# Products with zero weights ahead of TensorE's waits for a scores bank, in a two-layer transformer kernel on one core

## The chip, the cores and the metric

The kernel runs on 1 core of a Trainium2 chip. The metric is the device time of one execution in microseconds (us), as the median of several runs. One profiled execution of the kernel stands beside them: the hardware profiler records each instruction of each engine, with the clock that TensorE was granted. The engines are TensorE (PE in the profile, its weight loads PEld), VectorE (DVE), ScalarE (ACT), GpSimd (POOL) and SyncE (SP), which issues the transfers.

## What is computed

Four images of 1024 tokens with 128 features go through two layers. Each layer is a modulated layer norm, a causal attention with 16 heads of 8 features, a residual, a second modulated layer norm, a mixture of experts, and a residual. Cut to the attentions:

```python
# layer 0
Q, K, V = heads(h), heads(h @ Wk + bk), heads(h @ Wv + bv)   # V has 32 features a head
o = softmax(Q @ K.T + causal) @ V
x = x + ga * (h + gelu(o) @ Wf + bf)
# layer 1: q, k rotated; heads 0 to 5 plain, 6 to 9 hyperbolic, 10 to 15 on normalised q and k
out_a = softmax(q @ k.T / sqrt(8) + causal) @ v
inner = q @ k.T - tq * tk.T
dis   = sqrt(1 / curv) * arccosh(maximum(-curv * inner, 1 + 1e-7))
out_b = softmax(1 / (1e-6 + dis) + causal) @ v
out_c = softmax(sqrt(8) * qn @ kn.T + causal) @ v
```

## The kernel before

**Stages.** The program is a row of blocks, b = 0 to 5, with a barrier of all engines after each. Block b ends layer 1 of image b-2 (its experts), runs a joint attention, and then the rest of layer 0 of image b. In the joint attention the heads go in units of four. In block 0 it has the four units (0, 0) to (0, 3): layer 0 of image 0 alone. In blocks 1 to 3 it has seven units in the order (1, 0), (0, 0), (0, 1), (1, 1), (0, 2), (0, 3), (1, 2): the first number is the layer, and layer 1 belongs to the image before. In block 4 it has (1, 0), (1, 1), (1, 2). The text names a unit so, with its block. The four hyperbolic heads of layer 1 are a guest: its 24 half steps run between the steps of these units, in blocks 1 to 3 at every third step, in block 4 at every step from 2 to 25.

**Steps.** A unit has 12 steps, `STEPS`: a chunk `c` of 512 queries, a block `kb` of 128 keys, and the queries that are not masked, 512, 384, 256 or 128 wide. The widths of a unit's steps add up to 4608 columns. For each position p in the stage TensorE's program runs `scores(p + 1)`, then `values(p)`, then what is left of the side jobs, then, where the guest has a half step, `hyp_scores`.

- `scores` (L745) makes four bf16 products, two to a pair (L756). Each pair goes to two of the banks 0 to 3 of the accumulator memory. `take_banks` (L731) has TensorE wait until the pair of two jobs earlier has been read: by ScalarE's exponential (L1067), or, for a half step of the guest, by VectorE (L1375).
- `values` multiplies the exponentials in `pr` with the values into bank 4 (L797): four fp32 products on 32 columns of the array each, beside one another; the profile counts two MATMULs for each. The first key block of a chunk starts the sum, the last one (`kb == 4 * c + 3`) ends it, and VectorE then copies bank 4 out. In units of layer 0 four more products with a tile of ones put the row sums into bank 5 (L802).
- Side jobs stand between the scores and use the banks 6 and 7 in turn: the "pieces" of the row maxima of a later unit (L683, with the mask's product L686 on the diagonal), which VectorE reduces (L1311); the values of the guest (L714); transposes (L690, L697, L703, L726).

**What sets the order.** Each engine runs its program in the order written. TensorE has one queue: whatever stands behind a waiting product waits too. `side_plan` spreads the side jobs over the positions by their columns. `maskt` is the weight tile with the causal mask; TensorE transposes it once at the start, and VectorE makes the bf16 tile `maskqk` of it. `identb` is the identity in bf16.

Of the kernel before, what the change touches and what calls it, by code (L numbers as in the profile page):

```python
# [7 lines left out]
P = 128  # L8
# [15 lines left out]
HYP_EPS = 1e-06  # L24
NORM_EPS = 1e-24
HYP_UNIT = 3
LOW, HIGH = -3e38, 3e38

HEAD_ORDER = [12, 13, 14, 15, 4, 5, 10, 11, 0, 1, 2, 3, 6, 7, 8, 9]

F32, BF16 = mybir.dt.float32, mybir.dt.bfloat16
# [3 lines left out]
STEPS = []  # L35
# [4 lines left out]
NS = len(STEPS)  # L40
# [28 lines left out]
def layer(b, n):  # L69
    return 1 if n == HYP else UN[b][n][0]  # L70
# [39 lines left out]
NOBODY = -1  # L110
# [14 lines left out]
def hyp_at(b, p):  # L125

    return HYP_POS[b].index(p) if p in HYP_POS[b] else NOBODY
# [20 lines left out]
def std_steps(b):  # L148
    return NS * len(UN[b])
# [154 lines left out]
def adaln_kernel(nc, ins, out):  # L304
    with ExitStack() as ctx:
# [12 lines left out]
        w = {}  # L318
# [34 lines left out]
        weight("maskt", [P, P], ins["maskt"])  # L353
        weight("c", [P, 2 * B], ins["c"])
        cols = w["cols"]

        C_BK, C_BF, C_PB, C_QS, C_COS, C_BV = 0, 1, 2, 4, 5, 8

# [199 lines left out]
        def tensor_program(pe, b):  # L558
# [100 lines left out]
            def attention():  # L659
# [4 lines left out]
                def side_job(kind, g, what):  # L664
# [61 lines left out]
                            mm = pe.transpose(ps[:, bank, t * P:(t + 1) * P], o[:, t * P:(t + 1) * P], w["ident"][:])  # L726
                    mm.then_inc(J.side, 1)

                score_job = [0]

                def take_banks():  # L731

                    n = score_job[0]
                    score_job[0] += 1
                    if n == 0 and b >= 2:
                        pe.wait_ge(fs[1].x, NC)
                    if n >= 2:
                        hyperbolic, i, pair = JOBS[b][n - 2]
                        if hyperbolic:
                            pe.wait_ge(h_arg, i + 1)  # L740
                        else:
                            pe.wait_ge(J.exps, 2 * i + pair + 1)
                    return 2 * (n % 2)

                def scores(g, extra):  # L745
                    n, s = divmod(g, NS)
                    c, kb, q0, wd, diag = STEPS[s]
                    k = K_MAX if has_max(b, n) else PAIRS
                    o0 = q0 - c * CH
                    if s == 0 and has_max(b, n):  # L750
                        pe.wait_ge(J.maxrow[n], 48)
                    for pair in range(2):
                        bank = take_banks()
                        for j in range(2):
                            o = ps[:, bank + j, o0:o0 + wd]
                            mm = pe.matmul(o, kop[0:k, slot(n), 2 * pair + j, kb * P:(kb + 1) * P],  # L756
                                           qop[0:k, slot(n), 2 * pair + j, q0:q0 + wd], start=True, stop=True)
                            if j == 0 and extra and (pair or layer(b, n) == 0):
                                side_job(*extra.pop(0))
                        mm.then_inc(J.scores, 1)  # L760
                        if extra:
                            side_job(*extra.pop(0))
# [51 lines left out]
                for p in range(positions(b) + 1):  # L814
                    extra = jobs_at(p)
                    if p + 1 < steps:
                        scores(p + 1, extra)
                    if p < steps:
                        values(p)
                    for x in extra:  # L820
                        side_job(*x)
                    if hyp_at(b, p) != NOBODY:
                        hyp_scores(hyp_at(b, p))

            def output_projections():
# [1115 lines left out]
        with nc.Block() as block:  # L1941
# [70 lines left out]
            @block.vector  # L2012
            def _(dve):
                chain = [0]

                def link(i):
                    chain[0] += 1
                    i.then_inc(dve_chain, 1)
                    dve.wait_ge(dve_chain, chain[0])

                def modulation(l):
                    dve.wait_ge(s_mm, l + 1)
                    m = mod[:, l].rearrange("p j b -> p (j b)")
                    link(nc.vector.tensor_copy(m, ps[:, 6 + l, 0:6 * B]))
                    for j in (1, 4):
                        ins_ = nc.vector.tensor_scalar(mod[:, l, j], mod[:, l, j], 1.0, None, ALU.add)
                    ins_.then_inc(s_ready, 1)

                def gate_sign(l):
                    for j in (2, 5):  # L2030
                        g = mod[:, l, j]
                        link(nc.vector.tensor_scalar(nr[:, 0, 0:B], g, 0.0, 2.0, ALU.is_ge, ALU.mult))
                        link(nc.vector.tensor_scalar(nr[:, 1, 0:B], nr[:, 0, 0:B], -1.0, None, ALU.add))
                        link(nc.vector.tensor_scalar(nr[:, 2, 0:B], g, -1.0, None, ALU.mult))
                        link(nc.vector.tensor_tensor(nr[:, 0, 0:B], nr[:, 2, 0:B], g, ALU.max))
                        link(nc.vector.scalar_tensor_tensor(out=g, in0=nr[:, 0, 0:B], scalar=0.25,
                                                               in1=nr[:, 1, 0:B], op0=ALU.max, op1=ALU.mult))

                dve.wait_ge(s_first, firsts)
                nc.vector.reciprocal(hyp[:, 0:4], curvb[:]).then_inc(s_ready, 1)  # L2040
                nc.vector.tensor_scalar(consts[:, 6:7], cols[:, C_COS:C_COS + 1], -0.5, None, ALU.mult)
                nc.vector.tensor_copy(identb[:], w["ident"][:])
                dve.wait_ge(x_in, 16)
                for t in range(NT):
                    ins_ = nc.vector.bn_stats(st[:, t, :], xin[:, t, :])
                link(ins_)
                for t in range(NT):
                    ins_ = nc.vector.bn_aggr(mv[:, t, :], st[:, t, :])
                ins_.then_inc(ln_var[0], 1)
                y, z, v = sd[:, 0, :], sd[:, 1, :], mv[:, :, 1]  # L2050
                dve.wait_ge(ln_std[0], 1)
                link(nc.vector.tensor_tensor(z, y, y, ALU.mult))
                link(nc.vector.scalar_tensor_tensor(out=z, in0=v, scalar=LN_EPS, in1=z, op0=ALU.add, op1=ALU.mult))
                link(nc.vector.tensor_scalar(z, z, -0.5, 1.5, ALU.mult, ALU.add))
                link(nc.vector.tensor_tensor(z, z, y, ALU.mult))
                dve.wait_ge(ln_tok[1], 1)
                for t in range(NT):
                    nc.vector.tensor_scalar(xin[:, t, :], xin[:, t, :], mv[:, t, 0:1], sd[:, 1, t:t + 1],
                                            ALU.subtract, ALU.mult).then_inc(ln_norm[0], 1)
                modulation(0)  # L2060
                nc.vector.tensor_copy(maskqk[:], ps[:, 6, P:2 * P])
                for c in range(NC):
                    nc.vector.tensor_copy(chunk(xT(0), c), ps[:, c, :])
                gate_sign(0)
                modulation(1)
                gate_sign(1)
# [95 lines left out]
```

## Time and profile before

| | |
|---|---|
| median of 3 runs | 2625.94 us (2622.81 to 2629.74) |
| the profiled execution | 2617.08 us, span 2615.4 us |
| TensorE busy | 2163.1 us, 83% of the span |
| VectorE busy | 1485.9 us, 57% |
| ScalarE busy | 1354.2 us, 52% |
| GpSimd busy | 822.0 us, 31% |
| TensorE's clock granted | 0.821 of full on average |

The clock is granted at two levels, 1.2 and 2.4 GHz; a figure between 0.5 and 1 is the mix of both over a stretch, so that 2 x (1 - figure) is the share of the stretch at 1.2 GHz. The busy time of TensorE counts each product to the modelled end of its pipeline, so a busy TensorE is not yet one that streams at its peak. The profiled execution lies 8.9 us under the median.

### The profile page before, as it was taken

To read this page: it belongs to the slowest core of one execution; us is meant where nothing else is said; L and a number is where in the kernel's file an instruction comes from. 1 tells how busy PE (TensorE), PEld (TensorE's weight loads), DVE (VectorE), ACT (ScalarE), POOL (GpSimd) and SP (SyncE) were. 2 spreads that over 40 slices of the span, in tenths; PEclk is the share of its full clock that TensorE was granted. 3 is DMA by queue.
4 is the path that set the end of the run, shared out by engine and by line. 5 is a ranking of instruction groups with operands and counts; after the bars stand their busy time and mean duration, and the time that the engine had idled before them with its cause. 6 is when DMAs were issued, how large, how long until landed. Compare 5 with 4: busy or idle time off the path is not lost. (4 is left out here: it accounts for less than half of the span.)

```text
span 2615.4 us, 30040 instructions
## 1 busy us (share of the span) xinstructions
PE 2163.1 (83%) x10649; PEld 841.0 (32%) x10649; DVE 1485.9 (57%) x3046; ACT 1354.2 (52%) x1924; POOL 822.0 (31%) x918
## 2 busy tenths in 40 slices
PE   6898938888888499888898949988888868978779
PEld 2233412322224343222223424322222334422133
DVE  6562526667745454666763643576766444388542
ACT  2345415657773232657676422365777532278922
POOL 2112111333431243323342134232344113346624
PEclk7899956887888699687887969778788878976789
DMA  5000241111012242101102234201001223310032
GB/s 131 21 24 18 66 118 30 36 38 27 17 50 82 63 131 75 35 19 36 27 17 66 67 93 128 63 20 31 24 20 49 66 78 96 89 40 1 1 98 89
DMA packets 82104, 142.56 MB, mean 55 GB/s; under 512 B 11821, under 2 KB 34477, under 8 KB 77325
## 3 DMA queue, kind: packets, MB, share of 16 engines
q1 hardware_dynamic: 81954, 140.63, 19.1%
q8 instruction: 85, 1.39, 0.2%
q14 instruction: 65, 0.53, 0.1%
HBM read 124.22 MB, written 15.20 MB: 53 GB/s over the span
## 5 line engine op out<-in xcount | busy, mean ns | idle before, releaser
L1311 DVE TENSOR_REDUCE mx<-ps 128x1 f32<-128x512 f32 (+3 forms) x992 | 613.0, 655 | 281.7 <-PE ps L686 190.1
L1067 ACT ACTIVATE pr<-ps 128x1024 f32<-128x1024 f32 (+3 forms) x672 | 521.7, 804 | 416.0 <-PE ps L756 414.7
L683 PE MATMUL ps<-kop,qop 72*128 72x512 bf16 (+7 forms) x1248 | 447.6, 388 | 95.8 <-DVE mx L1311 69.3
L756 PE MATMUL ps<-qop,kop 75*128 75x512 bf16 (+7 forms) x1344 | 440.3, 383 | 88.2 <-DMA qop<-mrow 35.0
L797 PE MATMUL ps<-pr,vt 128*32 128x512 f32 (+3 forms) x2688 | 358.1, 612 | 10.8 <-POOL pr L1612 8.9
L1612 POOL TENSOR_SCALAR_AFFINE_SELECT pr<-pr 128x512 f32<-128x512 f32 x224 | 158.5, 708 | 617.9 <-ACT pr L1067 615.8
L1120 ACT ACTIVATE pr<-ps 128x512 f32<-128x512 f32 x224 | 133.7, 597 | 308.9 <-PE ps L881 242.9
L683 PEld LDWEIGHTS ps<-kop,qop 72*128 72x128 bf16 (+1 forms) x1248 | 131.4, 107 | 450.7 <-DVE mx L1311 288.6
L756 PEld LDWEIGHTS ps<-qop,kop 75*128 75x128 bf16 (+1 forms) x1344 | 130.7, 109 | 337.7 <-ACT pr L1067 103.0
L891 PE MATMUL ps<-pr,qop 128*128 128x512 f32 x384 | 194.6, 593 | 4.1 <-POOL pr L1603 4.1
L686 PE MATMUL ps<-maskqk,identb 128*128 128x128 bf16 x832 | 194.3, 256 | 0.0
L802 PE MATMUL ps<-pr,ones 128*32 128x512 f32 (+3 forms) x1536 | 178.6, 539 | 0.0
L1603 POOL TENSOR_TENSOR pr<-on,wb 128x512 f32<-128x512 f32 x84 | 106.3, 1265 | 129.1 <-DVE on L1539 123.3
L1539 DVE TENSOR_TENSOR on<-pr,ps 128x512 f32<-128x512 f32 x84 | 57.7, 687 | 149.0 <-ACT pr L1120 148.7
L878 PE MATMUL ps<-hT,kop 128*128 128x512 f32 x256 | 131.0, 593 | 4.3 <-DVE on L1539 4.3
L1375 DVE TENSOR_SCALAR wb<-ps 128x1024 f32<-128x1024 f32 (+3 forms) x96 | 91.6, 954 | 75.2 <-PE ps L770 61.3
L881 PE MATMUL ps<-hT,nbc 128*128 128x512 f32 x256 | 130.7, 592 | 0.0
L1365 DVE COPY osb<-ps 128x512 f32<-128x512 f32 x56 | 38.6, 689 | 127.1 <-PE ps L802 92.3
L891 PEld LDWEIGHTS ps<-pr,qop 128*128 128x128 f32 x384 | 72.3, 190 | 97.7 <-issue 83.1
L1702 POOL TENSOR_TENSOR wb<-wb 128x768 f32<-128x768 f32 (+2 forms) x42 | 76.3, 1816 | 78.7 <-ACT wb L1041 77.3
L686 PEld LDWEIGHTS ps<-maskqk,identb 128*128 128x128 bf16 x832 | 94.9, 114 | 18.5 <-issue 13.5
L797 PEld LDWEIGHTS ps<-pr,vt 128*32 128x32 f32 x2688 | 57.9, 118 | 127.2 <-issue 93.3
(332 smaller groups left out, 3076.9 us busy)
## 6 DMA issues: line engine op xcount, KB each, us to landing
wb<-gates_scratch SPq DMA_DIRECT2D x192, 256.0 KB, 3.3
kop<-kparts_scratch SPq DMA_DIRECT2D x32, 576.0 KB
qop<-qparts_scratch SPq DMA_DIRECT2D x96, 192.0 KB
nbc<-hmax_scratch SPq DMA_DIRECT2D x14, 512.0 KB, 4.3
xin<-in_x SPq DMA_DIRECT2D x7, 512.0 KB, 6.1
kparts_scratch<-on SPq DMA_DIRECT2D x12, 256.0 KB, 3.4
qparts_scratch<-on SPq DMA_DIRECT2D x12, 256.0 KB, 4.0
qparts_scratch<-wb SPq DMA_DIRECT2D x12, 192.0 KB
```

The source lines that it names most:

```text
L683: mm = pe.matmul(o, qop[0:k, slot(n), j, qb * P:(qb + 1) * P], kop[0:k, slot(n), j, k0:k0 + wd], start=True, stop=not diag)
L686: mm = pe.matmul(o[:, wd - P:wd], identb[:], maskqk[:], start=False, stop=True)
L756: mm = pe.matmul(o, kop[0:k, slot(n), 2 * pair + j, kb * P:(kb + 1) * P], qop[0:k, slot(n), 2 * pair + j, q0:q0 + wd], start=True, stop=True)
L797: mm = pe.matmul(ps[32 * j:32 * j + 32, 4, o0:o0 + wd], v, pr[:, g % 3, j, o0:o0 + wd], start=kb == 0, stop=last, tile_position=(0, 32 * j))
L802: mm = pe.matmul(ps[32 * j:32 * j + 32, 5, o0:o0 + wd], ones32[:], pr[:, g % 3, j, o0:o0 + wd], start=kb == 0, stop=last, tile_position=(0 ...
L878: mm = pe.matmul(ps[:, f.gate_banks[i % R], :], wt, h, start=True, stop=True)
L881: mm = pe.matmul(ps[:, 4 + i % 2, :], wt, h, start=True, stop=True)
L891: pe.matmul(ps[:, c, :], wt, fh[:, i % 3, :], start=i < NC, stop=i == f.last[c]).then_inc(g.down, 1)
L1067: nc.scalar.activation(pr[:, g % 3, 2 * pair:2 * pair + 2, o0:o0 + wd], ps[:, bank:bank + 2, o0:o0 + wd], ACT.Exp).then_inc(J.exps, 1)
L1120: nc.scalar.activation(fa[:, i % 3, :], ps[:, f.gate_banks[i % R], :], fn).then_inc(g.act, 1)
L1311: ins_ = nc.vector.tensor_reduce(mx[:, ring(b, n), j0:j0 + heads, qb, col % 2], ps[:, bank, 0:heads * wd].rearrange("p (j n) -> p j n", j= ...
L1612: nc.gpsimd.affine_select(past, past, [[0, 4], [1, P]], ALU.is_ge, 0.0, base=0, channel_multiplier=-1).then_inc(J.cut, 1)
```

## The change

The change adds matrix products that change no sum. Their weights are zeros: the memory of `maskt`, read as bf16 and cleared by VectorE after its only use. Their moving operand is `identb`, repeated to 512 columns. They add to bank 4, where the values' sum is open, so they stand only where the last values step was not the last of its chunk. There are two of them (`FILL`) ahead of each of the two pairs of a step of layer 1, one ahead of each pair of a step of layer 0 two positions after a half step of the guest, and one ahead of each half step of the guest. Block 0 has none.

```diff
@@
+FILL = 2
@@
+        zeros = w["maskt"][:].bitcast(BF16)[:, 0:P]
@@
+                def add_zeros(times):
+
+                    for _ in range(times):
+                        pe.matmul(ps[:, 4, :], zeros, identb[:].unsqueeze(1).broadcast_to([P, 4, P]),
+                                  start=False, stop=False)
+
+                def keep_busy(p, times):
+
+                    if 0 <= p < std_steps(b) and b:
+                        c, kb = STEPS[p % NS][:2]
+                        if kb != 4 * c + 3:
+                            add_zeros(times)
@@ def scores
                     for pair in range(2):
+                        if layer(b, n) or hyp_at(b, g - 2) != NOBODY:
+                            keep_busy(g - 2, FILL if layer(b, n) else 1)
                         bank = take_banks()
@@ position p
                     if hyp_at(b, p) != NOBODY:
+                        keep_busy(p, 1)
                         hyp_scores(hyp_at(b, p))
@@ VectorE, once at the start
-                nc.vector.tensor_copy(maskqk[:], ps[:, 6, P:2 * P])
+                link(nc.vector.tensor_copy(maskqk[:], ps[:, 6, P:2 * P]))
+                nc.vector.memset(zeros, 0.0)
```

TensorE's order at one full step of block 1, unit (1, 0), is this before; L756 are the scores, L683 the pieces, L797 the values:

```order
L683 MATMUL ps<-kop,qop 128x512
L756 MATMUL ps<-qop,kop 128x512 x2
L683 MATMUL ps<-kop,qop 128x512
L756 MATMUL ps<-qop,kop 128x512
L683 MATMUL ps<-kop,qop 128x512
L756 MATMUL ps<-qop,kop 128x512
L683 MATMUL ps<-kop,qop 128x512
L797 MATMUL ps<-pr,vt 32x512 x4
```

The same place in the changed program, where L734 is the product with zeros, L773 the scores, L685 the pieces and L814 the values:

```order
L685 MATMUL ps<-kop,qop 128x512
L734 MATMUL ps<-identb,w_maskt 128x512 x2
L773 MATMUL ps<-qop,kop 128x512 x2
L685 MATMUL ps<-kop,qop 128x512
L734 MATMUL ps<-identb,w_maskt 128x512 x2
L773 MATMUL ps<-qop,kop 128x512
L685 MATMUL ps<-kop,qop 128x512
L773 MATMUL ps<-qop,kop 128x512
L685 MATMUL ps<-kop,qop 128x512
L814 MATMUL ps<-pr,vt 32x512 x4
```

Four rows of 512 columns have come in, two ahead of each pair, and nothing else has moved.

In a unit of layer 0 of block 1 TensorE's order around a half step of the guest (L770) is this before, with the row sums at L802 and the guest's values at L714:

```order
L802 MATMUL ps<-pr,ones 32x512 x4
L683 MATMUL ps<-kop,qop 128x384
L686 MATMUL ps<-maskqk,identb 128x128
L770 MATMUL ps<-qop,kop 128x256 x2
L756 MATMUL ps<-qop,kop 128x512
L714 MATMUL ps<-wb,vt 32x384 x4
L756 MATMUL ps<-qop,kop 128x512
L683 MATMUL ps<-kop,qop 128x384
L686 MATMUL ps<-maskqk,identb 128x128
L756 MATMUL ps<-qop,kop 128x512
```

And in the changed program, where the guest's half step is L787:

```order
L819 MATMUL ps<-pr,ones 32x512 x4
L685 MATMUL ps<-kop,qop 128x384
L688 MATMUL ps<-maskqk,identb 128x128
L734 MATMUL ps<-identb,w_maskt 128x512
L787 MATMUL ps<-qop,kop 128x256 x2
L734 MATMUL ps<-identb,w_maskt 128x512
L773 MATMUL ps<-qop,kop 128x512
L716 MATMUL ps<-wb,vt 32x384 x4
L773 MATMUL ps<-qop,kop 128x512
L685 MATMUL ps<-kop,qop 128x384
L688 MATMUL ps<-maskqk,identb 128x128
L734 MATMUL ps<-identb,w_maskt 128x512
```

One row stands ahead of the half step and one ahead of the next pair; that pair was already the next thing in the queue. By the whole order the changed program has 610 of these products: 158 in each of the blocks 1 to 3 and 136 in block 4.

## Rows read from the trace of the kernel before

**Rows 1.** The page: TensorE's busy time, and its granted clock in 40 slices.

```profile
PE 2163.1 (83%) x10649; PEld 841.0 (32%) x10649; DVE 1485.9 (57%) x3046; ACT 1354.2 (52%) x1924; POOL 822.0 (31%) x918
...
PEclk7899956887888699687887969778788878976789
```

**Rows 2.** Windows, one a unit: block 0's (0, 1), then block 1's seven.

```profile
core 0: us, PE busy (x) PEld busy (x) DVE busy (x) ACT busy (x) POOL busy (x), PEclk, DMA share, GB/s
125.00:167.30 42.30, 39.41 (x322) 14.01 (x321) 25.97 (x47) 20.73 (x28) 7.63 (x10) 1.00 0.12 30
397.90:461.90 64.00, 53.40 (x260) 17.41 (x260) 43.63 (x76) 33.59 (x47) 14.49 (x15) 0.66 0.05 18
461.90:515.00 53.10, 47.22 (x343) 16.41 (x341) 36.48 (x66) 35.60 (x52) 18.89 (x26) 0.91 0.10 24
515.00:575.70 60.70, 50.65 (x374) 17.42 (x372) 40.73 (x79) 35.61 (x56) 17.36 (x23) 0.92 0.14 38
575.70:634.40 58.70, 47.79 (x261) 15.71 (x253) 43.08 (x68) 43.58 (x51) 23.55 (x21) 0.78 0.09 21
634.40:694.50 60.10, 52.96 (x354) 17.46 (x357) 41.69 (x66) 43.95 (x52) 23.20 (x22) 0.84 0.13 30
694.50:746.80 52.30, 47.72 (x340) 16.15 (x333) 36.54 (x61) 38.16 (x53) 21.34 (x27) 0.88 0.08 22
746.80:776.20 29.40, 27.02 (x178) 7.09 (x176) 6.71 (x20) 25.10 (x42) 10.56 (x19) 0.77 0.38 108
```

**Rows 3.** Windows: block 2's (1, 0), (0, 1), (1, 1), (1, 2); block 3's (1, 0), (1, 1).

```profile
1022.10:1089.20 67.10, 56.74 (x269) 18.55 (x268) 44.95 (x78) 33.43 (x45) 14.49 (x15) 0.67 0.14 41
...
1141.00:1207.10 66.10, 56.71 (x374) 19.18 (x372) 41.28 (x79) 35.73 (x57) 17.38 (x23) 0.82 0.13 35
1207.10:1271.30 64.20, 53.35 (x269) 17.39 (x261) 45.56 (x68) 43.79 (x52) 23.14 (x21) 0.70 0.08 20
...
1381.50:1410.90 29.40, 28.20 (x178) 7.27 (x176) 6.65 (x19) 25.03 (x41) 10.25 (x18) 0.71 0.38 108
1657.10:1725.00 67.90, 57.59 (x269) 19.14 (x268) 45.26 (x78) 33.43 (x45) 14.48 (x15) 0.64 0.14 40
...
1841.70:1900.70 59.00, 49.35 (x261) 16.96 (x253) 43.11 (x68) 43.47 (x51) 23.95 (x21) 0.75 0.08 21
```

**Rows 4.** Windows: block 4's (1, 0), (1, 1), (1, 2).

```profile
2283.60:2354.00 70.40, 54.19 (x264) 17.19 (x265) 56.42 (x96) 50.97 (x79) 30.49 (x34) 0.72 0.12 39
2354.00:2445.10 91.10, 70.69 (x319) 21.11 (x317) 75.70 (x104) 82.88 (x97) 59.27 (x47) 0.61 0.00 1
2445.10:2483.80 38.70, 30.43 (x198) 7.70 (x190) 14.32 (x35) 36.37 (x58) 20.92 (x31) 0.79 0.00 0
```

**Rows 5.** Windows: steps 4 to 6 of unit (1, 1), block 1, then block 2.

```profile
594.50:606.20 11.70, 10.40 (x61) 3.23 (x60) 10.07 (x16) 11.53 (x13) 4.15 (x3) 0.85 0.00 1
1225.90:1243.90 18.00, 17.25 (x71) 5.11 (x63) 13.18 (x17) 11.97 (x14) 3.74 (x3) 0.52 0.00 1
```

**Rows 6.** What TensorE waited for in block 1's joint attention: total, times, longest.

```profile
PE ps L683 <- DVE mx L1311: 17.0, 37, 1.5
PE ps L756 <- DVE wb L1375: 7.2, 10, 1.2
PE ps L756 <- DMA qop<-mrow: 7.2, 4, 2.7
PE ps L756 <- ACT pr L1067: 5.2, 8, 1.3
```

**Rows 7.** TensorE's timeline in block 1's (1, 1): start, length, line.

```profile
601.87 0.38 PE L683 MATMUL ps<-kop,qop 72*128 72x512 bf16 x1
602.09 0.38 PE L756 MATMUL ps<-qop,kop 75*128 75x512 bf16 x1
...
603.04 1.07 PE L797 MATMUL ps<-pr,vt 128*32 128x512 f32 x8
604.04 0.28 PE L683 MATMUL ps<-kop,qop 72*128 72x256 bf16 x1
```

**Rows 8.** The same timeline in block 2's (1, 1).

```profile
1230.05 0.63 PE L683 MATMUL ps<-kop,qop 72*128 72x512 bf16 x1
1230.48 0.63 PE L756 MATMUL ps<-qop,kop 75*128 75x512 bf16 x1
```

## The prediction

> **What bounds the kernel now.** I read the page first. TensorE is busy for 83% of the span, far more than any other engine, so the kernel is TensorE's nearly everywhere. But its granted clock is 0.821 on average, and in the 40 slices it is lowest in the joint attentions of the blocks from 1 on (6 to 8 tenths) and in a few phases where other engines work [rows 1]. Next I cut the attentions into units by the windows view and looked at the clock column. Block 0's attention, layer 0 alone, holds 1.00. In block 1 the units of layer 0 have 0.84 to 0.92, those of layer 1 only 0.66 and 0.78, and the last unit 0.77 [rows 2]. Blocks 2 and 3 repeat this: 0.67 and 0.64 for (1, 0), 0.70 and 0.75 for (1, 1) [rows 3]. In block 4 the figures are 0.72, 0.61 and 0.79, but there ScalarE is busy 82.88 us of 91.1 in the longest unit [rows 4]. So in blocks 1 to 3 TensorE sets the pace together with VectorE, which it feeds with pieces, and in block 4 it is mostly ScalarE.
>
> Does the clock matter for the time? The same work recurs at other clocks, and this is the best view of the case. Time at the low clock is 2 x (1 - clock) x length. Unit (1, 1) took 58.7 us with 25.8 us of it at the low clock in block 1, and 64.2 us with 38.5 us in block 2 [rows 2, 3]: 5.5 us more for 12.7, or 0.43 us for each. Unit (0, 1) gives (66.1 - 60.7) / (23.8 - 9.7) = 0.38. Three steps alone took 11.7 us at clock 0.85 and 18.0 us at 0.52 with the same work [rows 5]: 6.3 us for 13.8, or 0.46. Unit (1, 0) gives less, (67.9 - 67.1) / (48.9 - 44.3) = 0.17, and the last unit nothing: 29.4 us at 0.77 and at 0.71, with ScalarE busy 25.1 us of it. I take 0.4 for each us at the low clock, 0.3 in unit (1, 0), 0 in the last unit.
>
> Which waits are there? In the whole attention of block 1 TensorE is idle for 17.0 us on VectorE's reductions, and ahead of scores (L756) for 7.2 us on VectorE's read for the guest, 5.2 us on ScalarE and 7.2 us on a transfer; no wait exceeds 2.7 us [rows 6]. So the waits for a scores bank are few. What the zero products can bring is the clock, not the waits.
>
> **What a product with zeros costs.** It is a bf16 product of 512 columns, as the pieces and scores are. Two such stand 0.22 us apart at the full clock (601.87 to 602.09) [rows 7] and 0.43 us at the low one (1230.05 to 1230.48) [rows 8]. It waits for nothing, needs no other engine, and delays what stands behind it in TensorE's queue: a pair of scores, then a piece. The 158 of a block fall as follows, by the rule on `kb` and the guest's places: 38 in (1, 0), 43 in (1, 1), 41 in the last unit, 36 in the four units of layer 0.
>
> How much of that delay reaches the time? A comparison bounds it from below. A unit of layer 0 has the row sums' products on top of what a unit of layer 1 has: about as long as the values' own, which take 1.00 us in a full step with the changeover (603.04 to 604.04) [rows 7]. At 4608 columns, nine full steps' worth, that is 8 to 9 us a unit. Brought to the full clock by the prices above, the four units of layer 0 in block 1 take 49.3, 56.8, 52.4 and 47.3 us, mean 51.4; (1, 1) takes 48.4 and (1, 0) 51.0, mean 49.7 [rows 2]. So 8 to 9 us of more work on TensorE cost 1.7 us: one fifth. The cover is VectorE, busy 43 us of a unit's 59 to 64, and ScalarE. The upper bound is everything. The zeros stand ahead of the scores, which feed ScalarE, where the row sums stand behind the values and feed nobody at once; so I double the fifth and take 0.4.
>
> **Term A, (1, 0) and (1, 1) of blocks 1 to 3: the clock.** Four zero products in a step are 0.88 us, which is what the row sums add to a step of layer 0. So I forecast for these units the clock that layer 0's have, 0.88 (0.82 to 0.92 in rows 2 and 3). At 60 us that leaves 14.4 us at the low clock in each. Now it is 43.5, 44.3 and 48.9 us in (1, 0), together 136.7, and 25.8, 38.5 and 29.5 in (1, 1), together 93.8 [rows 2, 3]. The fall is 93.5 x 0.3 = 28 us and 50.6 x 0.4 = 20 us: -48 us.
>
> **Term B, their zeros.** 81 a block, 243 in three, x 0.22 = 53.5 us of TensorE; x 0.4 = +21.4 us (between 10.7 and 53.5).
>
> **Term C, layer 0's units of blocks 1 to 3.** 108 x 0.22 = 23.8 us. These units are nearer to TensorE's bound, so half of it, +11.9 us. At the low clock are 9.6 + 9.7 + 19.2 + 12.6 = 51 us in block 1 [rows 2]; I take the same for each block, and a quarter of it to go, since only every third step has zeros: 153 x 0.25 x 0.4 = -15.3 us. Together -3.4 us.
>
> **Term D, the last unit of blocks 1 to 3.** 41 zeros, 9 us of TensorE in a unit of 29.4 us that the clock doesn't move. ScalarE covers nearly all; I take a tenth of 27 us, +3 us (0 to 27).
>
> **Term E, block 4.** 136 x 0.22 = 30 us, covered by ScalarE and VectorE: a tenth, +3 us. At the low clock are 39.4, 71.1 and 16.3 us [rows 4], 127 in all; two thirds of it may go, at a price between 0 (as in the last unit) and 0.4. The longest unit can win at most the 8.2 us that ScalarE is idle in, so I take 0.1: -8.4 us. Together -5.4 us.
>
> **The start.** VectorE now waits for its cast of the mask and clears 128 x 64 words, once. The trace has no such clear; it lies between nothing and a few tenths of a us, and I take +0.3.
>
> Sum: -48 + 21.4 - 3.4 + 3 - 5.4 + 0.3 = -32 us. Against the profiled execution's 2617.1 us that is 2585; against the median of 2625.9, to which the result will be compared, 2594 us.
>
> The Trainium skill, in "TensorE: Matmul & The Clock Gate", section "HAM oscillation — how this bites in real kernels", makes the clock fall after TensorE has been idle for one whole period of the monitor. By that rule fillers in a queue without long gaps can't help. The trace speaks against it: TensorE waits at most 2.7 us at a time in block 1's attention [rows 6] and is busy 53.4 us of 64.0 at clock 0.66 [rows 2]. The same page's next section, "A second HAM failure mode: psum-queue depth-cycling", says that short idles between groups of products make the clock go up and down, and that fits these rows. By the first rule the result is that of the first rival below, by the second that of the forecast.
>
> **Rivals.**
> - *The clock doesn't answer* to products with zeros, or not to work of this kind; the zeros are pure load. At the mix of clocks now they cost about 0.35 us in layer 1's units and 0.25 in layer 0's: 243 x 0.35 x 0.4 = 34, 108 x 0.25 x 0.5 = 13.5, and a tenth of 123 x 0.3 and 136 x 0.35, 8.5. That is +56 us, 2682 us. For it: busy shares of 83% and more at low clocks, so being busy alone doesn't raise it [rows 2]. Against it: the units with the row sums have the higher clock in every block. Chance 0.12.
> - *The zeros hold up what VectorE and ScalarE wait for.* The clock rises as forecast, but each zero product delays the next pair and the piece behind it in full. All 610 at 0.22 us are 134 us, against gains of 48 + 15 + 8 = 72: +62 us, 2688 us. It decides from an exposed share of 0.54 on. For it: VectorE and ScalarE are fed through the same queue; against it: the fifth measured on the row sums. Chance 0.08.
> - *Half a clock.* The low clock shrinks to 0.80 in layer 1's units, 24 us in each: 65 x 0.3 + 22 x 0.4 = 28 us of gain, less 21.4, and no gain in C and E beyond their cost: about -7 us, 2619 us. For it: the last steps of a chunk, and those after them, get no zeros, and unit (1, 0) has waits which zeros don't fill. Chance 0.15.
> - *More than forecast.* The full clock in layer 1's units with a fifth exposed: 137 x 0.4 + 94 x 0.43 = 95 us, less 11, and C to E as above: some -90 us, 2536 us. Chance 0.05.
>
> **How the numbers follow.** The forecast has 0.60, with its own range 2562 to 2616 (exposed share 0.2 to 0.6, clock 0.84 to 0.92). What a measurement of this kernel can tell from no change is about 0.3%, or 8 us. Faster takes the forecast (0.60), more than forecast (0.05) and a third of the half clock (0.05): 0.70. Same takes most of the rest of the half clock and the edge of the forecast's cases: 0.12. Slower takes the first two rivals, less a part that ends near zero: 0.18. The range that leaves out the two dear rivals' centres and the far gain is 2552 to 2640 us.
>
> **What would show it.** In the changed kernel's windows: the clock of (1, 0) and (1, 1) in blocks 1 to 3 near 0.88, their lengths shorter by some 4 to 5 us each net; the last unit at 29 to 31 us whatever its clock; block 0 as before, its clock 1.00. In the waits, less idle time of TensorE ahead of pieces, more of VectorE on TensorE. The forecast is wrong if the clock of these units stays at 0.64 to 0.78 (first rival), or if it rises and the units don't shorten (second). Then ScalarE's and VectorE's waits for TensorE's scores and pieces would have grown.

## The result, and the profile after

The changed kernel took 2608.61 us (median of 4 runs, 2604.3 to 2611.8), the kernel before in the same comparison 2624.55 us. The ratio is 0.9935, with a 95% interval of 0.9914 to 0.9956: 0.65% or 17 us faster, between 12 and 23 (the two medians lie 15.9 us apart). The forecast was 32 us. The profiled execution of the changed kernel took 2611.8 us, its span is 2610.1 us.

From the page of the changed kernel, the busy times and the granted clock in 40 slices:

```profile
PE 2178.3 (83%) x11259; PEld 889.0 (34%) x11259; DVE 1490.6 (57%) x3047; ACT 1355.6 (52%) x1924; POOL 817.8 (31%) x918
...
PEclk7899957988999599998899869898899968988879
```

610 more products stand on TensorE, 134 us of them at 0.22 us each, and its busy time has grown by only 15 us [rows 1]. The others stream faster: the mean clock of the profiled executions went from 0.821 to 0.875.

The windows of the changed kernel, one a unit: block 1's seven, then (1, 0), (0, 0), (1, 1) and (1, 2) of block 2, then block 4's three. They answer to [rows 2, 3, 4].

```profile
398.00:466.80 68.80, 59.21 (x306) 22.73 (x306) 43.82 (x76) 33.72 (x47) 14.07 (x15) 0.74 0.05 16
466.80:516.40 49.60, 44.18 (x350) 15.64 (x342) 36.48 (x66) 35.60 (x52) 18.87 (x26) 1.00 0.10 26
516.40:579.40 63.00, 54.52 (x375) 19.08 (x376) 40.99 (x79) 35.75 (x56) 17.37 (x23) 0.89 0.14 37
579.40:637.40 58.00, 50.07 (x309) 19.17 (x308) 43.10 (x68) 43.67 (x52) 23.20 (x21) 0.89 0.08 22
637.40:695.20 57.80, 51.42 (x367) 17.66 (x366) 42.37 (x66) 43.55 (x52) 23.92 (x22) 0.90 0.14 31
695.20:746.50 51.30, 46.83 (x347) 17.00 (x340) 36.72 (x61) 38.19 (x53) 21.46 (x28) 0.93 0.08 22
746.50:777.40 30.90, 29.50 (x217) 10.12 (x215) 6.54 (x21) 25.18 (x41) 10.26 (x18) 1.00 0.38 103
1025.50:1090.10 64.60, 54.03 (x316) 21.51 (x314) 45.12 (x79) 33.68 (x45) 13.60 (x15) 0.88 0.15 42
...
1090.10:1141.20 51.10, 45.51 (x341) 16.12 (x342) 36.43 (x66) 35.60 (x52) 18.86 (x26) 0.97 0.10 25
...
1204.10:1262.00 57.90, 49.55 (x300) 18.83 (x292) 43.09 (x68) 43.58 (x51) 23.21 (x21) 0.89 0.09 22
1371.30:1402.20 30.90, 29.50 (x217) 10.10 (x215) 6.53 (x21) 25.18 (x42) 10.12 (x18) 1.00 0.37 103
2272.30:2342.20 69.90, 54.41 (x310) 20.40 (x311) 57.65 (x96) 50.85 (x78) 30.29 (x34) 0.89 0.12 39
2342.20:2432.40 90.20, 68.73 (x360) 23.48 (x359) 74.36 (x104) 82.85 (x96) 58.56 (x48) 0.80 0.00 1
2432.40:2475.60 43.20, 37.36 (x240) 11.51 (x238) 14.29 (x35) 36.47 (x58) 20.30 (x30) 0.90 0.00 1
```

Read the column PEclk first: layer 1's units stand at 0.88 and 0.89 where they had 0.67 and 0.70 in block 2, and the last unit at 1.00. Only (1, 0) of block 1 stays low, at 0.74. The lengths follow only in part. In block 2, (1, 0) is 2.5 us shorter and (1, 1) 6.3, the last unit 1.5 us longer. In block 4 the last unit grew from 38.7 to 43.2 us.

TensorE's timeline in a full step of the changed kernel's (1, 1) of block 2 shows one reason:

```profile
1231.25 0.39 PE L685 MATMUL ps<-kop,qop 72*128 72x512 bf16 x1 [0.37 <-DVE mx L1329]
1231.47 0.60 PE L734 MATMUL ps<-identb,w_maskt 128*128 128x512 bf16 x2
1231.91 0.60 PE L773 MATMUL ps<-qop,kop 75*128 75x512 bf16 x2
1232.34 0.38 PE L685 MATMUL ps<-kop,qop 72*128 72x512 bf16 x1
1232.56 0.60 PE L734 MATMUL ps<-identb,w_maskt 128*128 128x512 bf16 x2
1232.99 0.38 PE L773 MATMUL ps<-qop,kop 75*128 75x512 bf16 x1
```

The products with zeros (L734) are where the order put them. Two take 0.44 us (1231.47 to 1231.91), 0.22 each as forecast. But the scores behind them start the moment they end, and so does everything up to 1232.99: there was no wait for a bank for them to fill. In such a step TensorE is the path.

The waits of TensorE in block 1's attention (total, times, longest), which answer to [rows 6]:

```profile
PE ps L685 <- DVE mx L1329: 18.4, 37, 1.5
PE ps L773 <- ACT pr L1085: 4.9, 10, 1.3
PE ps L773 <- DMA qop<-mrow: 4.0, 2, 2.2
...
PE ps L773 <- DVE wb L1393: 1.4, 3, 0.7
```

The wait on VectorE's read for the guest went from 7.2 to 1.4 us: some of the added products stand in such waits and cost nothing there. That on VectorE's reductions grew by 1.4 us.

Added up over the whole span, the two profiled executions differ so:

| part | forecast | before | changed | difference |
|---|---|---|---|---|
| (1, 0) and (1, 1), blocks 1 to 3 (terms A, B) | -26.6 | 381.0 | 371.7 | -9.3 |
| layer 0's units, blocks 1 to 3 (C) | -3.4 | 683.3 | 669.6 | -13.7 |
| the last units, blocks 1 to 3 (D) | +3 | 88.1 | 94.2 | +6.1 |
| block 4's attention (E) | -5.4 | 200.2 | 203.3 | +3.1 |
| everything else | +0.3 | 1262.8 | 1271.4 | +8.6 |

The single parts are less sure than the whole. The execution profiled before was 9 us faster than its median and the changed one 3 us slower. What lies outside the joint attentions, where the program adds nothing but the clear at the start, takes 1103.8 to 1116.0 us in the profiled executions of all kernels of this study.

### The profile page after: what moved, and what is told of

Read it like the earlier page. It is cut to its first block and busy times, and to the rows that moved or that the text cites. A ratio compares the mean times of both kernels' runs of the same rounds, so it can differ in the third digit from the quotient of the medians.

```text
span 2610.1 us, 31253 instructions
## 1 busy us (share of the span) xinstructions
PE 2178.3 (83%) x11259; PEld 889.0 (34%) x11259; DVE 1490.6 (57%) x3047; ACT 1355.6 (52%) x1924; POOL 817.8 (31%) x918
## 5 line engine op out<-in xcount | busy, mean ns | idle before, releaser
L685 PE MATMUL ps<-kop,qop 72*128 72x512 bf16 (+7 forms) x1248 | 418.4, 364 | 98.7 <-DVE mx L1329 73.4
L773 PE MATMUL ps<-qop,kop 75*128 75x512 bf16 (+7 forms) x1344 | 408.9, 353 | 50.2 <-ACT pr L1085 17.7
L814 PE MATMUL ps<-pr,vt 128*32 128x512 f32 (+3 forms) x2688 | 314.7, 542 | 6.7 <-POOL pr L1630 4.9
L685 PEld LDWEIGHTS ps<-kop,qop 72*128 72x128 bf16 (+1 forms) x1248 | 127.8, 104 | 406.1 <-DVE mx L1329 285.7
L734 PE MATMUL ps<-identb,w_maskt 128*128 128x512 bf16 x610 | 212.8, 414 | 16.7 <-DMA qop<-mrow 16.7
L773 PEld LDWEIGHTS ps<-qop,kop 75*128 75x128 bf16 (+1 forms) x1344 | 129.7, 103 | 260.9 <-issue 66.7
L688 PE MATMUL ps<-maskqk,identb 128*128 128x128 bf16 x832 | 184.6, 245 | 0.0
L819 PE MATMUL ps<-pr,ones 128*32 128x512 f32 (+3 forms) x1536 | 165.2, 502 | 0.0
L1654 POOL TENSOR_SCALAR sd<-mv 128x4 f32<-128x4 f32 x30 | 6.9, 229 | 287.3 <-DVE mv L1195 220.3
```

Source lines behind the costliest of these rows:

```text
L685: mm = pe.matmul(o, qop[0:k, slot(n), j, qb * P:(qb + 1) * P], kop[0:k, slot(n), j, k0:k0 + wd], start=True, stop=not diag)
L688: mm = pe.matmul(o[:, wd - P:wd], identb[:], maskqk[:], start=False, stop=True)
L734: pe.matmul(ps[:, 4, :], zeros, identb[:].unsqueeze(1).broadcast_to([P, 4, P]), start=False, stop=False)
L814: mm = pe.matmul(ps[32 * j:32 * j + 32, 4, o0:o0 + wd], v, pr[:, g % 3, j, o0:o0 + wd], start=kb == 0, stop=last, tile_position=(0, 32 * j))
L819: mm = pe.matmul(ps[32 * j:32 * j + 32, 5, o0:o0 + wd], ones32[:], pr[:, g % 3, j, o0:o0 + wd], start=kb == 0, stop=last, tile_position=(0 ...
```

## The experiments

Each kernel is the changed one with the edit shown. The ratios are to the kernel before, with their 95% intervals; 0.9935 is the changed kernel's. All added products leave the sums as they are, so every kernel computes the whole output.

**Is it the streaming?** Each product cut to 8 columns:

```diff
-                        pe.matmul(ps[:, 4, :], zeros, identb[:].unsqueeze(1).broadcast_to([P, 4, P]),
-                                  start=False, stop=False)
+                        pe.matmul(ps[:, 4, 0:8], zeros, identb[:, 0:8], start=False, stop=False)
```

> The changed kernel with its 610 products with zeros cut from 512 to 8 columns; the instructions and their places stay. Theory 1 (the products pay by keeping TensorE streaming, which lifts the granted clock): the clock falls back to about 0.82 and the time to the kernel before's, ratio 1.000 within 0.003, unit (1, 1) of block 2 back near 64 us. Theory 2 (the products pay by the instructions themselves or by where they shift the queue, the clock being incidental): the ratio stays at 0.993 or falls below.

Measured: 1.0028 (1.0001 to 1.0055), median clock of its ten runs 0.8145 against 0.816 before. Two windows of (1, 1), blocks 2 and 3:

```profile
1222.30:1281.70 59.40, 48.93 (x304) 17.50 (x292) 43.26 (x68) 43.60 (x52) 23.59 (x21) 0.77 0.09 21
1864.00:1929.50 65.50, 55.63 (x300) 18.88 (x292) 45.57 (x68) 43.94 (x51) 23.15 (x21) 0.67 0.08 19
```

The same 610 instructions in the same places bring nothing when they stream next to nothing. Clock and gain are gone together. Theory 2 is refuted. But block 2's (1, 1) took 59.4 us and not the 64 expected, block 3's 65.5: one unit of one execution is a poor measure.

**Which products carry it?** Only the pairs' products of layer 1:

```diff
-                        if layer(b, n) or hyp_at(b, g - 2) != NOBODY:
-                            keep_busy(g - 2, FILL if layer(b, n) else 1)
+                        if layer(b, n):
+                            keep_busy(g - 2, FILL)
...
-                        keep_busy(p, 1)
```

> Only the two products ahead of each pair of layer 1's units (116 a block); those at the guest's half steps and in layer 0's units are left out. The changed kernel took 14 us off layer 0's units of blocks 1 to 3 where I had put 3. If that came from the 36 products in them, it is gone here: ratio about 0.998. If it came from the phase in which layer 0's units are entered (the clock's state left by the unit before), most of it stays: 0.994.

Measured: 0.9983 (0.9958 to 1.0009), clock 0.8665. By the profiled execution, the four units of layer 0 take 230.3, 227.0 and 228.4 us in the blocks 1 to 3; before it was 226.2, 228.0 and 229.1, and 221.7, 223.2 and 224.6 in the changed kernel. Without the 36 products in these units the 14 us are gone, as the first reading had it. But the 14 us don't stand firm: the sum of the three blocks is 683.3 us before and 669.6 in the changed kernel, and in other kernels below that keep the 36 products it is 672.0 to 685.0 in their profiled executions.

Only the single products:

```diff
-                        if layer(b, n) or hyp_at(b, g - 2) != NOBODY:
-                            keep_busy(g - 2, FILL if layer(b, n) else 1)
+                        if layer(b, n) == 0 and hyp_at(b, g - 2) != NOBODY:
+                            keep_busy(g - 2, 1)
```

> Only the single products, 42 in each of blocks 1 to 3 and 20 in block 4; none ahead of layer 1's pairs. Theory 1: layer 0's units in blocks 1 to 3 keep a clock over 0.90 and are 3 to 5 us a block shorter than before, units (1, 0) and (1, 1) are at 0.65 to 0.78 as before, and the last units are back to 29.4 us (38.8 in block 4), since their products cost 1.5 and 4.4 us: ratio 0.993 to 0.996. If the two per pair carry the gain, the ratio is 0.998 to 1.000.

Measured: 0.9963 (0.9929 to 0.9997), clock 0.8295: 146 products, a quarter of them, bring some half of the gain by the ratio. The interval is wide, and the two medians differ by only 3.9 us. The windows of the last units of blocks 1 and 2, and of (1, 1) of block 2:

```profile
746.80:775.80 29.00, 25.71 (x179) 7.00 (x177) 6.66 (x19) 24.96 (x41) 10.75 (x19) 0.82 0.41 110
1384.60:1411.00 26.40, 24.30 (x179) 6.56 (x177) 6.74 (x19) 24.60 (x41) 9.79 (x17) 0.87 0.44 120
1210.10:1275.00 64.90, 54.00 (x264) 18.40 (x256) 45.63 (x68) 44.02 (x51) 23.05 (x21) 0.69 0.08 19
```

(1, 1) is back at 0.69 and 65 us, as expected. Layer 0's units come to 226.3, 226.6 and 225.4 us, only 1 us a block or so under before, where 3 to 5 had been expected. By these executions either kind alone gives them little; whether both together give more isn't shown, since the 14 us are one execution.

**What does a product cost where it can't bring anything?** Two ahead of each pair of block 0 as well, at a clock that is 1.00 already:

```diff
-                    if 0 <= p < std_steps(b) and b:
+                    if 0 <= p < std_steps(b):
...
-                        if layer(b, n) or hyp_at(b, g - 2) != NOBODY:
-                            keep_busy(g - 2, FILL if layer(b, n) else 1)
+                        if layer(b, n) or b == 0 or hyp_at(b, g - 2) != NOBODY:
+                            keep_busy(g - 2, FILL if layer(b, n) or b == 0 else 1)
```

> The changed kernel, with two products ahead of each pair in block 0 as well (156 more, 34 us at 0.22 us each). There the clock is 1.00 already, so that only their price shows. If a fifth to two fifths is exposed, as taken in the prediction, block 0's units (0, 1) and (0, 2) grow from 41.6 us by 2 to 4 us and the whole by 7 to 14 us; if TensorE's queue is the path there, they grow by 8 to 9 us each and the whole by about 30 us.

Measured: 0.9982 (0.9958 to 1.0006). The windows of block 0's (0, 1), (0, 2), (0, 3):

```profile
129.80:176.00 46.20, 45.87 (x363) 18.40 (x362) 26.39 (x47) 21.09 (x29) 7.64 (x10) 1.00 0.12 27
176.00:222.10 46.10, 45.76 (x362) 18.36 (x361) 26.39 (x47) 20.99 (x28) 7.63 (x10) 1.00 0.09 24
222.10:256.30 34.20, 33.79 (x272) 11.68 (x274) 1.38 (x2) 20.65 (x28) 7.01 (x9) 1.00 0.01 2
```

In the kernel before, (0, 2) and (0, 3) took:

```profile
167.30:208.90 41.60, 39.47 (x322) 14.01 (x321) 25.98 (x47) 20.77 (x29) 7.63 (x10) 1.00 0.10 27
208.90:236.10 27.20, 25.96 (x234) 7.99 (x236) 1.38 (x2) 20.13 (x28) 7.01 (x9) 1.00 0.01 2
```

So 40 products cost 4.5 us in (0, 2), 0.11 us each or half of their 0.22. In (0, 3), which has no pieces for VectorE, they cost 7.0 us, 0.18 each or four fifths. (0, 1) grew by 3.9 us. The expectations for these two units were 2 to 4 and 8 to 9 us each, so the first nearly held there, and it held for the whole: 0.9982 against 0.9935 is 12 us. This is the purest price of the study.

**Without them in the last units:**

```diff
-                    if 0 <= p < std_steps(b) and b:
+                    if 0 <= p < std_steps(b) and b and p < std_steps(b) - NS - 2:
```

> The changed kernel without the products of the last unit of blocks 1 to 4. There they cost: 29.4 became 30.9 us (32.4 once) and 38.8 became 43.2 us, while with single products alone these units took 26.4 to 29.0 and 40.5 us. Theory 1: the last units fall to 27 to 29 us and to 39 to 41, the rest stays, the whole is 8 to 14 us under the changed kernel, ratio 0.989 to 0.991. Rival: the products keep the clock up into the phases that follow, whose time grows by as much; ratio 0.993 to 0.995.

Measured: 0.9898 (0.9861 to 0.9934), as theory 1 had it for the whole, some 10 us under the changed kernel. The intervals overlap; on the same chip the kernel with zeros by zeros (below), which has the changed kernel's products, had a median of 2608.96 us and this one 2596.35. The profiled last units of blocks 1 to 3 and of block 4:

```profile
748.30:779.80 31.50, 30.16 (x178) 7.80 (x176) 6.70 (x20) 25.31 (x42) 10.48 (x19) 0.67 0.36 101
1376.30:1402.90 26.60, 24.46 (x178) 6.51 (x176) 6.67 (x20) 24.84 (x41) 10.52 (x19) 0.87 0.43 119
1997.30:2028.90 31.60, 28.66 (x178) 7.71 (x176) 6.69 (x20) 25.27 (x42) 10.73 (x19) 0.73 0.36 101
...
2429.10:2468.60 39.50, 33.54 (x198) 7.99 (x190) 14.31 (x35) 36.58 (x58) 20.92 (x32) 0.69 0.00 1
```

The same work takes 26.6 us at 0.87 and 31.5 at 0.67. The last unit does answer to the clock. It fell to the 27 to 29 us expected in block 2 alone; in blocks 1 and 3 it lost the clock with the products and took 31.5 and 31.6. Blocks 1 to 3 together have 89.7 us here, 94.2 in the changed kernel and 88.1 before. (1, 1) of block 4 took 85.2 us at 0.88, where the changed kernel's profile has 90.2 at 0.80 with one product more.

**How many?** First one ahead of each pair, then four:

```diff
-FILL = 2
+FILL = 1
```

> FILL = 1: one product ahead of each pair of layer 1's units, half the load. Theory 1 with the price measured in block 0 (0.115 us of time for each): the price falls by 58 a block and about 6 us a block; if one product is enough to hold the clock of (1, 1) over 0.85 the ratio is about 0.987, if the clock falls back to 0.75 or so it is 0.993 to 0.996.

> FILL = 4. The clock of the units (1, 0) and (1, 1), already 0.88 and 0.89, can rise by 0.1 at most, about 12 us less at the low clock, worth 3 to 5 us a unit; two times 40 more products cost a unit 9 us at the price of block 0, up to 17 us if TensorE's queue is then the path. Units (1, 0) and (1, 1) grow by 4 to 12 us each, the whole by 40 us or more: ratio 1.01 to 1.02.

Measured: 0.9896 (0.9861 to 0.9931) with one and 1.0161 (1.0114 to 1.0209) with four; clock 0.864 and 0.891. One is better than two by 10 us, between the two cases expected; the intervals overlap, but three of the four executions with one lie under all ten of the kernel with zeros by zeros on the same chip. In the profiled execution the clock of (1, 1) fell back in two blocks (0.78 and 0.76, 62.0 us) and not in the third (0.96, 53.9 us). Four raise the clock little and make it dear. Their whole came as expected, by other units than expected: (1, 1) of blocks 1 to 3 grew by only 3 us, under the 4 to 12, and the last units by 5 to 9. The last unit of block 2 with one:

```profile
1379.20:1407.00 27.80, 25.62 (x198) 8.42 (x196) 6.82 (x21) 24.85 (x41) 10.28 (x19) 1.00 0.42 114
```

and that of block 1 with four, with (1, 1) of block 3:

```profile
747.40:785.60 38.20, 37.55 (x255) 13.90 (x253) 6.54 (x21) 25.75 (x42) 10.02 (x18) 1.00 0.30 83
1857.30:1917.80 60.50, 53.92 (x358) 21.88 (x356) 43.40 (x68) 44.03 (x51) 23.00 (x21) 1.00 0.08 21
```

The last unit's rows are at clock 1.00, and so is the changed kernel's at 30.9 us: 27.8 us with one, 30.9 with two, 38.2 with four. The 20 products from one to two cost 0.16 us each, the 40 from two to four 0.18. With one it takes 27.8 us in all three blocks; with none it took 29.3 to 29.4 before, and 31.5, 26.6 and 31.6 in the kernel above.

**Do the data matter?** Zeros as the moving operand too:

```diff
-                        pe.matmul(ps[:, 4, :], zeros, identb[:].unsqueeze(1).broadcast_to([P, 4, P]),
+                        pe.matmul(ps[:, 4, :], zeros, zeros.unsqueeze(1).broadcast_to([P, 4, P]),
```

> The changed kernel with zeros as the moving operand too, in place of the repeated identity: no operand bit changes in the added products. If the granted clock follows the streaming alone, clock (0.88 in units (1, 0) and (1, 1)) and time (ratio 0.993) stay; if it follows what the data switch, the clock of these units falls back toward 0.65 to 0.78 and the time to 1.00 or above.

Measured: 0.9934 (0.9911 to 0.9957), clock 0.879 against 0.8785. (1, 1) of block 1 and (1, 0) of block 2:

```profile
580.80:636.30 55.50, 46.88 (x320) 18.13 (x318) 43.01 (x68) 43.73 (x51) 23.35 (x21) 0.99 0.10 23
1024.10:1088.10 64.00, 53.04 (x316) 20.89 (x314) 45.11 (x79) 33.56 (x45) 13.62 (x15) 0.89 0.15 43
```

Nothing changed: zeros streamed against zero weights hold the clock as well as the identity does. The weights are zeros in both kernels, so products that switch real data in the array were not tried.

**Did (1, 0) gain?** No products in it:

```diff
-                        if layer(b, n) or hyp_at(b, g - 2) != NOBODY:
+                        if UN[b][n] != (1, 0) and (layer(b, n) or hyp_at(b, g - 2) != NOBODY):
...
-                        keep_busy(p, 1)
+                        if p >= NS:
+                            keep_busy(p, 1)
```

> The changed kernel without any added product in the units (1, 0) of blocks 1 to 4 (38 fewer in each of blocks 1 to 3, more in block 4). The prediction put 28 us of gain less 10 of price into these units of blocks 1 to 3; the changed kernel showed 1 us. Theory 1a (a long part of (1, 0) isn't paced by TensorE, so that its clock pays little there): these units stay at 64 to 68 us as before and as with the products, and the whole is within 5 us of the changed kernel, ratio 0.992 to 0.995. Theory 1b (the products there also hold the clock for the unit behind them): unit (0, 0), 49.6 to 51.1 us with them, goes back to 52 to 53 us. Rival (the unit did gain, and the profiled executions hid it by chance): the whole loses 10 us or more, ratio 0.997 or above.

Measured: 0.9979 (0.9964 to 0.9994), clock 0.853. (1, 0) and (0, 0) of blocks 2 and 3:

```profile
1026.10:1094.00 67.90, 57.59 (x269) 19.14 (x268) 45.28 (x78) 33.45 (x45) 14.51 (x15) 0.64 0.14 40
1094.00:1147.10 53.10, 48.79 (x351) 17.24 (x350) 36.78 (x66) 35.62 (x51) 18.88 (x26) 0.91 0.10 24
1661.70:1733.60 71.90, 63.63 (x270) 21.12 (x268) 45.65 (x78) 33.47 (x45) 14.51 (x15) 0.56 0.14 38
1733.60:1789.00 55.40, 51.39 (x351) 17.84 (x350) 36.75 (x66) 35.74 (x51) 18.95 (x26) 0.86 0.10 23
```

With the products these were 64.6, 51.1, 64.5 and 51.0 us. Over blocks 1 to 3 the products save 8 us in (1, 0) and 9 us in (0, 0), which has only single products of its own: it is entered at a higher clock. In its first 5 us the clock is 0.50 in all three blocks here, with TensorE busy the whole 5 us, and 1.00, 0.76 and 0.76 in the changed kernel. The ratios differ by 0.0044, 12 us, with the intervals apart. Theory 1a fell, with its 5 us; 1b held, and so did the rival that (1, 0) itself gained and single executions hid it. How much they can hide: (1, 0) of block 1 runs from 61.0 us (the kernel with half as wide products) to 68.9 (8 columns), and was 63.9 in the profile before.

**Streaming or number?** Half as wide, as many:

```diff
-                        pe.matmul(ps[:, 4, :], zeros, identb[:].unsqueeze(1).broadcast_to([P, 4, P]),
+                        pe.matmul(ps[:, 4, 0:256], zeros, identb[:].unsqueeze(1).broadcast_to([P, 2, P]),
```

> The changed kernel with each added product cut from 512 to 256 columns: as many products, half the streaming. FILL = 1 had half as many pair products at full width and gave 0.9896. If streaming time sets both what the products bring and what they cost, this gives 0.988 to 0.991 as well; if the price is by the product, it stays at 0.993.

Measured: 0.9901 (0.9885 to 0.9918), clock 0.857, as one of full width (0.9896, 0.864). (1, 1) of block 1 and the last unit of block 2:

```profile
571.40:626.90 55.50, 45.48 (x300) 19.03 (x292) 42.92 (x68) 43.30 (x51) 23.54 (x21) 0.89 0.09 23
...
1363.10:1390.80 27.70, 25.53 (x217) 9.96 (x215) 6.91 (x21) 24.78 (x41) 10.30 (x18) 1.00 0.42 115
```

At the full clock the last unit takes 27.7 us with two halves, 27.8 with one whole and 30.9 with two. At 0.89 (1, 1) takes 55.5 us with 43 halves and 57.9 to 58.0 with 43 whole ones: 2.4 us for what is 21.5 whole products, 0.11 each. The price is by the column.

**A better version.** Two only in (1, 1):

```diff
-                            keep_busy(g - 2, FILL if layer(b, n) else 1)
+                            keep_busy(g - 2, FILL if UN[b][n] == (1, 1) else 1)
```

> One product ahead of each pair of layer 1's units, but two in (1, 1), from the unit table: (1, 1) took 62, 62 and 54 us with one and 57.9 us with two, the last unit 27.8 with one and 30.9 with two, (1, 0) about 65 with either. (1, 1) goes to 56 to 58 us, the others stay as with one: 3 to 6 us a block under FILL = 1's 0.9896, in blocks 1 and 2 at least, ratio 0.985 to 0.988. If the profiled executions' (1, 1) was chance, the ratio is 0.989 again.

Measured: 0.9849 (0.9825 to 0.9872), median 2592.32 us against 2629.43: faster than the kernel before by 1.5% and than the changed one by 0.9%, intervals apart. From one product everywhere (0.9861 to 0.9931) it isn't told apart; (1, 1) did what was expected, 55.9 and 55.7 us in blocks 1 and 2 where one product had 62.0. (1, 1) of block 2 and of block 4:

```profile
1202.10:1257.80 55.70, 46.83 (x320) 18.35 (x318) 43.04 (x68) 43.80 (x52) 23.38 (x21) 0.98 0.09 22
...
2332.80:2418.10 85.30, 63.88 (x360) 21.18 (x359) 70.64 (x104) 82.78 (x97) 59.95 (x46) 0.88 0.00 1
```

## Why the prediction was right, and where its sizes were off

**The mechanism was right.** The waits for a bank were few before and are not what paid. The clock was. Cut to 8 columns the products bring nothing, and the clock of (1, 0) and (1, 1) came to 0.88 and 0.89, where 0.88 was forecast (but 0.74 in (1, 0) of block 1). The rival of a clock that doesn't answer is refuted. So is the Trainium skill's first rule, in "TensorE: Matmul & The Clock Gate", section "HAM oscillation — how this bites in real kernels", as a full account of this kernel: the clock was at 0.66 in a unit of an attention where TensorE never waited over 2.7 us [rows 2, 6], and more streaming raised it. The next section's account, short idles between groups, fits.

**The sizes were not.** The change is half of the forecast, 17 us for 32, and it came out on the forecast's side because two terms were wrong in opposite directions. That is luck as far as the price goes. One sign failed plainly: (1, 0) and (1, 1) were to be 4 to 5 us shorter each, and in the profiled executions they are some 1.5 us shorter on average, at the clock that was forecast.

**The gain was sized too small, by an estimate.** The kernel before gives it: its own executions differ in clock. In 31 of them on one chip the clock runs from 0.806 (2643.93 us) to 0.822 (2608.07 us), and a straight line through them has 15 us for each 0.01; two other sets of 17 executions give 17 and 10. One hundredth is 52 us at the low clock, so that is 0.3 us for each, near the 0.3 and 0.4 taken. The median clock rose by 0.0625, from 0.816 to 0.8785, or 330 us less at the low clock, where terms A, C and E had 266. At 15 us that is 94 us (63 to 106 by the other two slopes), against 72 forecast. This carries a line four times beyond the clocks that it was drawn through. The ten executions of the kernel with zeros by zeros, at 0.870 to 0.883, lie on a line of 10 us, so the low end may be nearer.

**The price failed.** Terms B, C, D and E put 21.4 + 11.9 + 3 + 3 = 39 us on the 610 products. The measured change is 17 us, so by that estimate the price is 94 - 17 = 77 us, 0.13 us each (0.08 to 0.15 by the other slopes). The runs show it directly where the clock is the same with or without: 0.10 to 0.18 us in block 0, 0.11 to 0.13 in (1, 1), 0.16 and 0.18 in the last unit. At 0.12 for the 351 products of (1, 0), (1, 1) and layer 0's units and 0.17 for the 123 of the last units, blocks 1 to 3 alone come to some 63 us, where B, C and D had 36. Of the steps of the prediction these were mis-sized:
- "I take 0.4" in term B rested on a comparison of units of layer 0 and 1. Those have other side jobs beside them, and the comparison was made after both had been brought to the full clock by rough prices. In (1, 1), from two products at 0.99 (55.5 us, in the kernel with zeros by zeros) to four at 1.00 (60.5 us in block 3), 40 products cost 5.0 us, 0.125 each: 0.57 is exposed, not 0.4. The units of terms A and B say the same: at the prediction's own 0.3 and 0.4 the clocks of the changed kernel's rows give 43 us, 9.3 were measured, and 34 are left for 243 products, 0.14 each.
- "ScalarE covers nearly all" in term D was wrong. I read 25.1 us busy of 29.4 and equal lengths at 0.77 and 0.71 as a unit that TensorE doesn't pace. The same unit takes 26.6 us at 0.87 and 31.5 at 0.67, and its products beyond one a pair cost 0.16 to 0.18 us each. In the changed kernel it is 1.5 us longer at the full clock in blocks 1 and 2, and 3 us at 0.90 in block 3.
- Term E had -5 us for block 4. Its three units went from 200.2 to 203.3 us, 4.5 us of it more in the last unit, where the cover of a tenth was wrong as in term D. (1, 1) took 91.1 us before and 90.2 at clock 0.80, but with the same 50 products in other kernels it took 87.5, 89.1 and 94.0 us: what the products do there stays open.
- The price of the clock in (1, 0), 0.17 and then 0.3, was read from blocks 2 and 3 alone. Block 1 had 64.0 us with nearly block 2's low clock (43.5 against 44.3 us) [rows 2, 3], so these rows gave no price.

The price lies in the queue, as the second rival had it, at an exposed share of 77 / 134 = 0.57 (0.34 to 0.66 by the other slopes), about its 0.54. With the gain of 94 us it would have had to be over 0.70 for the change to lose time. What kept the result on the fast side is that the gain was larger too.

**Whole balance.** The same working for the other kernels takes 15 us for each 0.01 over 0.816. The counts are from the order of each kernel, the clocks are medians of its runs, and the price is what is left, so the table spreads one estimate over all and tests nothing by itself:

```
                    products   clock    gain   measured   price each
thin8                  610     0.8145     -2      +7        0.01
guest_only             146     0.8295     20     -10        0.07
layer1_pairs           464     0.8665     76      -4        0.15
no_first_unit          452     0.853      55      -6        0.11
not_last               444     0.8665     76     -27        0.11
one_per_pair           378     0.864      72     -27        0.12
two_halves        610 halves   0.857      61     -26        0.06
two_in_the_middle      458     0.8725     85     -40        0.10
changed                610     0.8785     94     -17        0.13
zero_times_zero        610     0.879      94     -17        0.13
block0_too             766     0.8815     98      -5        0.12
four_per_pair         1074     0.891     112     +42        0.14
```

Beside the 8 columns and the halves the prices run from 0.07 to 0.15, near the 0.10 to 0.18 measured directly. From two to four the clock gives 0.0125 and the 464 products take everything back. What stays open is what each kind of product does for layer 0's units: the spread between executions is of the size of these differences, and I did not separate them.

## What to carry to other kernels

Where TensorE's granted clock is low in stretches that TensorE paces, added products can pay, but they are paid for by the column. The best placement here brought 1.5%. Look for the fewest that hold the clock, unit by unit, and price one where the clock is full already: about half of it was on the path beside a busy VectorE, four fifths where VectorE was idle. Stop where one more costs more than the clock still gives: in the last units one a pair already had the full clock and 27.8 us, and the second made it 30.9.

Executions of one unchanged kernel can serve as the experiment: the same step at two clocks gives the price of the clock before anything is built. Take many of them, since a single pair (29.4 us at 0.77 and 0.71) said that the last unit didn't care, and don't trust the line far beyond the clocks that it was drawn through. The lengths of single units in one profiled execution are as weak a witness afterwards: the 14 us that layer 0's units seemed to gain did not come again.

## What the runs showed of the hardware that I had not expected

- The mean granted clock differs between executions of the same kernel, 0.806 to 0.822 in 31 of them, and the time with it, 2643.93 to 2608.07 us. The correlation is -0.84 (-0.86 and -0.71 in two other sets of 17), so most of this kernel's spread goes with the clock.
- A unit's length and clock recur. (1, 1) with the same 43 products took 57.9 or 58.0 us at 0.89 in eight of the 18 units that six profiled executions have of it, and 55.9 us at 0.97 in six.
- The profile shows TensorE busy for all of 5 us at a clock of 0.50, as in the first 5 us of (0, 0) when (1, 0) ahead of it had no products.
- Products of zeros by zeros raise the granted clock as much as those of zeros by an identity: 0.879 against 0.8785, ratio 0.9934 against 0.9935.
- Products of 8 columns, 610 of them, leave the clock about where it was (0.8145 against 0.816) and cost at most little: 1.0028, that is 7 us, between 0 and 14.
